# A new pacing condition for the expert-weight loads: from scatters sent to weights split

## The reference

```
logits = xf @ w_cls.T ; scores = softmax(logits)          # 32 routed experts + 32 that do nothing
topk_idx = top_k(scores + bias, 8) ; w = scores[topk] / sum * 1.5
for each routed expert e (at most 256 tokens of its own):
    g, u = split(x_e @ w_gate_up[e])                        # 512 -> 2 x 256
    y_e  = (silu(g) * u) @ w_down[e]                        # 256 -> 512
out[token] += w * y_e[token] * (1 + weight of the experts that do nothing)
```

## Time and profile before

| what | value |
|---|---|
| profiled execution, its own time | 969.67 us |
| its span | 967.9 us |
| mean granted TensorE clock | 0.98 of full speed |
| DMA moved over the span | 127.06 MB |
| HBM read, written | 106.53 MB, 32.90 MB |
| VectorE, ScalarE, GpSimd busy | 80%, 52%, 50% of the span |

### The profile page before, as it was taken

How to read it: one execution, slowest core, us unless ns; L and a number is a source line. 1 busy time by engine, 2 the same in 40 slices (tenths; PEclk the granted TensorE clock), 3 DMA queues, 4 the chain that set the end, 5 groups by cost and what they waited for, 6 DMA issues and landing times. The chain is left out here.

```text
span 967.9 us, 14567 instructions
## 1 busy us (share of the span) xinstructions
PE 904.0 (93%) x4362; PEld 731.9 (76%) x4362; DVE 772.4 (80%) x1843; ACT 503.1 (52%) x867; POOL 481.9 (50%) x395
## 2 busy tenths in 40 slices
PE   4789999999999999999988999999997699999995
PEld 3667888888888888888857888888875567777783
DVE  6968888888888898888887777777777598888882
ACT  5445545555545555455565323223322488787782
POOL 2457656667666676566650000000003458688852
PEclk9979999999999999999999999999998799999999
DMA  8001111111111111110275377444228589899932
GB/s 312 6 22 61 39 50 59 46 49 39 61 49 45 49 61 39 50 59 35 83 277 195 123 266 261 143 154 151 70 70 284 155 255 331 280 336 281 323 42 38
DMA packets 67369, 127.06 MB, mean 131 GB/s; under 512 B 12073, under 2 KB 14505, under 8 KB 65233
## 3 DMA queue, kind: packets, MB, share of 16 engines
q1 hardware_dynamic: 58144, 114.67, 33.8%
q0 software_dynamic: 9136, 11.31, 6.4%
HBM read 106.53 MB, written 32.90 MB: 144 GB/s over the span
## 5 line engine op out<-in xcount | busy, mean ns | idle before, releaser
L595 POOL TENSOR_TENSOR a_t<-a_t 128x512 f32<-128x512 f32 x80 | 105.0, 1313 | 102.8 <-DVE a_t L358 102.8
L604 POOL TENSOR_TENSOR a_fQ<-a_fQ,a_den 128x512 f32<-128x512 f32 x64 | 87.9, 1374 | 71.9 <-DVE a_den L396 71.9
L213 PE MATMUL a_PQ<-w_h,a_xT_h 128*128 128x512 f32 x384 | 107.8, 403 | 10.3 <-DVE w_l L345 9.6
L782 PE MATMUL r_PY<-w_h,r_o_h 128*128 128x512 f32 x256 | 105.8, 413 | 3.4 <-DVE r_o_l L884 3.4
L1070 POOL TENSOR_SCALAR r_vr<-r_mv 128x1 f32<-128x1 f32 x16 | 8.4, 525 | 196.7 <-DVE r_mv L895 196.7
L213 PE MATMUL a_PQ<-w_l,a_xT_h 128*128 128x512 f32 x384 | 105.3, 397 | 0.0
L213 PE MATMUL a_PQ<-w_h,a_xT_l 128*128 128x512 f32 x384 | 103.4, 391 | 0.0
L1214 POOL DMA_INDIRECT m_xg<-xn2d,si x64 | 81.4, 1272 | 40.3 <-issue 18.2
L782 PE MATMUL r_PY<-w_h,r_o_l 128*128 128x512 f32 x256 | 101.1, 395 | 0.0
L782 PE MATMUL r_PY<-w_l,r_o_h 128*128 128x512 f32 x256 | 100.5, 393 | 0.0
L392 DVE CUSTOM_DVE_ANT_0 a_m<-a_fQ,a_z 128x128 f32<-128x128 f32 x256 | 100.4, 444 | 0.0
(11 more groups left out here) (182 smaller groups left out, 2243.4 us busy)
## 6 DMA issues: line engine op xcount, KB each, us to landing
oT<-a_o SPq DMA_DIRECT2D x64, 256.0 KB, 2.4
v_l<-in_wgu SPq DMA_DIRECT2D x32, 512.0 KB
raw<-in_wgu SPq DMA_DIRECT2D x24, 512.0 KB
v_l<-oT SPq DMA_DIRECT2D x11, 1024.0 KB, 7.0
v_l<-in_wd SPq DMA_DIRECT2D x16, 512.0 KB
raw<-in_wd SPq DMA_DIRECT2D x12, 512.0 KB
v_h<-oT SPq DMA_DIRECT2D x5, 1024.0 KB, 6.1
out<-r_x SPq DMA_DIRECT2D x18, 256.0 KB, 2.0
```

What stands on the lines that cost most here:

```text
L213: last = eng.matmul(bank[:, :], a[:, k, :], w[:, 4 * i + k, :], start=s == 0 and k == 0, stop=s == 2 and k == 3)
L595: eng.tensor_tensor(t1[:, r % 2, :], t1[:, r % 2, :], t2[:, r % 2, :], ALU.add).then_inc(sm["xr"], 1)
L604: eng.tensor_tensor(q, q, den[:, n % 2, :].unsqueeze(2).broadcast_to([P, 4, P]), ALU.mult).then_inc(sm["fs"], 1)
L782: last = eng.matmul(PY[c % 2][:, :], a[:, c % 2, h * P:(h + 1) * P], b[:, h, :], start=h == 0 and s == 0, stop=h == NH - 1 and s == 2)
```

## The change

SyncE no longer waits for `m_sent`, and GpSimd no longer counts it. In its place every part of every load from expert 8 on waits for `m_wl >= 3(e-5) + part + 1`: VectorE has split the same part of expert `e-5`. The waits for the slot's former user stay. Parts, sizes, order and number of the transfers stay.

```
@@ -1192,8 +1192,7 @@
                     for part in range(3):
                         for t in range(2):
                             eng.wait_ge(sm[f"m_gu{t}" if part < 2 else f"m_yd{t}"], e - RING + 1)
-                        if e >= RING + 2:
-                            eng.wait_ge(sm["m_sent"], e - RING - 1)
+                        eng.wait_ge(sm["m_wl"], 3 * (e - RING + 3) + part + 1)
                         if part < 2:
                             load_up(sm, eng, ring, wgu, e, (part,))
                         else:
@@ -1216,15 +1215,14 @@
-                def scatter(e, t, rows, done, last):
+                def scatter(e, t, rows, done):
                     i = 2 * e + t
                     if t == 0 and e >= 1:
                         eng.wait_ge(sm["m_s"], 32 * e)
                     eng.wait_ge(sm[f"m_y{t}"], e + 1)
                     eng.indirect_dma_start(
                         out[:, :], bass.IndirectOffsetOnAxis(ap=si[0:rows, i:i + 1], axis=0),
-                        y[0:rows, e % 4, t, :], None, compute_op=ALU.add,
-                        engine_sem=sm["m_sent"] if last else None).then_inc(sm["m_s"], done)
+                        y[0:rows, e % 4, t, :], None, compute_op=ALU.add).then_inc(sm["m_s"], done)
@@ -1237,10 +1235,10 @@
                     with eng.If_lt(regs[e % 7], T):
-                        scatter(e, 0, P, 16, False)
-                        scatter(e, 1, P, 16, True)
+                        scatter(e, 0, P, 16)
+                        scatter(e, 1, P, 16)
                     with eng.Else():
-                        scatter(e, 0, 64, 32, True)
+                        scatter(e, 0, 64, 32)
```

## The result

The changed kernel takes 978.83 us (median of 4 runs, 972.0 to 981.46); the kernel before, run beside it, 969.08 us (median of 4, 962.09 to 969.67). The ratio of after to before is 1.0119, with a 95% interval of 1.0069 to 1.0169: slower by about 1.2%, where I had forecast 969.4 us and no change. This ratio is not the quotient of the two medians (1.0101): it rests on 20 executions of the changed kernel, 971.63 to 984.93 us, with a 21st of 986.47 us left out as slow. The ratios of the experiments are formed in the same way, each against the kernel before as it ran beside them. The profiled execution took 979.09 us, its span is 977.3 us.

A forecast was written before the change was run, and what follows sets the result against it. The bound was a 5.58 us ring of dependences per expert iteration, without transfers, nearly filled by TensorE's work. From 969.67 us, minus 0, 0, 0 and 0.3, came 969.4 us; range 966.8 to 971.8.

The forecast's parts named there:

- I take 0 for the increment: GpSimd's scatters lose the `m_sent` increment: cost 0, at most a few hundredths of a microsecond for each of 32 scatters.
- the 4.89 us between scatters 8 and 9: On GpSimd, scatter 9 starts 4.89 us after scatter 8, read as released by scatter 8's landing.
- 0.69 us to spare: Slack per expert claimed for the chain of scatters: the iteration's 5.58 us minus 4.89.
- Rival C: Scatters fall behind as spread parts lengthen landings by 1.5 us, until `y` buffers run out: 972.5 us, chance 0.13.
- The page estimate: Scatters meeting HBM's loaded latency, 1.8 us more each, would give 979.1 us; given a small part of Rival C's chance.
- The removed wait of SyncE: Dropping SyncE's wait for `m_sent`: worth 0 to TensorE, since that queue runs 29 us ahead of its reader.
- The added wait: SyncE's `m_wl` wait delays loads 1.3 to 5 us steadily, up to 19 us at the start; hidden by cover, cost 0.
- The startup: Load 8 leaves the stretch 756 to 760 us, where ScalarE and TensorE idle: gain taken as 0.3 us.
- rival B: Without load 8 the startup's 2.50 us "remote" wait shrinks, TensorE resumes up to 2.7 us sooner: 967.0 us, chance 0.20.
- The sign that I had set: Prediction is wrong if the iteration's length changes at all or the stretch 750 to 780 changes by over 1.9 us.

The follow-up runs named there:

- e3_counted: The changed kernel, but its scatters still count `m_sent`, for which nobody waits: 965.88 us, ratio 0.998.
- e1_both: The kernel before with the new `m_wl` wait added to the old `m_sent` wait: 965.16 us, ratio 0.9987.
- e9_counted_nopace: The kernel before without any pacing wait on SyncE, its scatters still counting `m_sent`: 961.47 us, ratio 0.9979.
- e7: The kernel before with the scatter's two waits swapped, so the landing wait is an instruction of its own: 974.65 us, ratio 1.0152.
- e5: The changed kernel with `m_sent` still counted and the scatter's two waits swapped, the landing wait its own instruction: 986.76 us, ratio 1.0279.
- e10_even_counted: The changed kernel, but only scatters of even experts count `m_sent`, for which nobody waits: 967.13 us, ratio 1.0017.

## Why the prediction was wrong

**The step that failed** is "On GpSimd the scatter loses one increment and keeps its descriptors ... I take 0 for the increment". Its bound, a few hundredths of a microsecond for each scatter, priced the increment as work. As work it costs nothing that can be seen: the last scatters take 1.43 us with it and without. What it does is let a scatter of 64 rows go without the wait for `m_s` that is on it. Without it, each scatter is held for the landing before, 3.84 us behind its predecessor at the end instead of 2.10. That turned a chain that follows the copies into one of 5.7 to 7.5 us a step beside an iteration of 5.58.

**The reading under it failed too.** I took the 4.89 us between scatters 8 and 9 in the earlier trace rows as a landing, since the bracket names one. But scatter 9 starts 0.86 us after its copy ends, as scatter 31 does after its own (0.81 us, with nothing landed). The timeline of ACT before:

```profile
825.15 0.60 ACT L1415 ACTIVATE m_y<-m_PY 128x512 f32<-128x512 f32 x1
```

The copies of experts 8 and 9 are 5.84 us apart (819.31 and 825.15), and scatter 8 lagged 0.95 us more behind its copy (1.81 us, behind a gather) than scatter 9. 5.84 minus 0.95 are the 4.89 us, and the "0.69 us to spare" of the landing chain was a number of nothing. The real step under load stood in none of my rows, because the counted scatters don't show it.

**Rival C had the path and not the cause.** I gave it 0.13 and priced it at 972.5 us. It named the resource that ran out, the four `y` buffers. It left the lag 15.0 us to grow; measured it grew by 18.3, from 4.2 to 22.5, with iterations that had grown longer by then. Its rate was close: 0.81 us per expert forecast, measured (22.5 minus 4.2) over the 17 experts from 2 to 19, which is 1.08. Its mechanism was wrong: not a landing that grows because the parts lie over the scatters (e3_counted has the same parts and no loss) but the landing being waited for at all. And its price left out two followers: the gathers behind the scatters on GpSimd, which cost TensorE 8.0 us of waits where `y` cost ScalarE 3.4, and the 5.2 us at the end, which are paid whatever the slack.

**The page estimate** of 979.1 us by the Trainium skill (DMA: Bandwidth & Descriptors, section Latency and other measured facts) lies 0.3 us from the median and is right by luck: it needs a rise of the landing time from the one pacing to the other, and e3_counted shows no loss from the pacing.

**The removed wait of SyncE**, taken at 0 because its reader is 29 us behind: right in this kernel (e1_both, e3_counted and e9_counted_nopace are all at 1.00). It is right only because the scatters ran free. With a real landing wait the same removal costs 1.3% (e7 against e5). I had argued from the load's cover alone and not from what else a held load may do, for which the likely candidate is to leave the DMA engines to the scatter.

**The added wait**, steady and at the start, taken at 0: right, with its times to 0.2 us. **The startup**, 0.3 us or rival B's 2.7: the steady part of the changed kernel starts 5.7 us earlier, but the load is not the reason. Some 2.4 us of it lie ahead of everything that the change touches: the first gather of the experts starts at 736.16 us after and at 738.54 before. The wait that rival B wanted shortened stands in e3_counted, where load 8 goes out at 774.03 and not in this stretch (timeline of ACT):

```profile
757.68 0.60 ACT L1379 ACTIVATE m_xT_h<-m_PX 128x512 fp32r<-128x512 f32 x1 [2.45 <-remote]
```

Before, it was 2.50 us. And the pair of scatters of expert 1 comes at 780.10 us before, at 780.03 in e3_counted, which has the new issues, and at 770.08 in e7, which has the old ones. What sets this stretch stays open; each is one execution. The sign that I had set, that the prediction is wrong if the stretch from 750 to 780 changes by over 1.9 us, was met, but not through the change.

**What stays open**: how the wait for `m_s` is dropped, by the chip or by what loads the program onto it, why the one for `m_y1` is not, and whether it always is. One counted scatter of the kernel before, that of expert 2 at 789.36, stood for 2.83 us and started 2.9 us behind its copy, which I can't explain. It is no accident of one execution: the same scatter stands 1.36 us in e1_both, 1.84 in e3_counted, 2.70 in e9_counted_nopace and 1.48 in e10_even_counted. It is the first scatter of 64 rows and follows a pair of 128; there the wait may have held. Seen are the start of the scatter, its packets and the time. The landing wait is there to keep two scatters from adding to the same row at once. At the end of the kernel before the packets of scatter 31 still come after all 80 of scatter 30; whether that always holds under load, with rows shared by neighbouring experts, was not tried. So the kernel before and all that are as fast owe part of their time to a safeguard that is written down and not kept; the changed kernel keeps it.

## What to carry to other kernels

An increment or a wait on an instruction is not priced by its own duration: before one is removed, look whether the instructions that carry it behave like those that don't, here whether the scatter starts before its predecessor's packets have landed. A releaser named beside a short idle time is a guess; check it against the other input of the instruction (a constant 0.8 us behind the copy says copy) and against the packets. And when something in an in-order queue falls behind by a constant amount per iteration, the price is what runs out first, the buffers, the queue's other work and the end, each by itself.

## What the runs showed of the hardware

An accumulating scatter of 64 rows by GpSimd that carries a wait for the landing semaphore and, beside its landing increment, a second increment by the engine, started though the wait was not met: 2.10 us behind its predecessor, against 3.83 to 3.95 us without that increment. A scatter of 128 rows with the second increment that carries a wait for a semaphore of ScalarE did wait: it started 0.27 us after the copy. The Trainium skill (Perfetto Trace Analysis, section DMA Instruction — SWDGE (GPSIMD)) lists the semaphores being satisfied before such an instruction goes to its engine; the kernels without the second increment agree (3.84 us), those with it do not where the wait is for the landing. The same section says that whether surplus semaphore updates are supported there is not known; here the kernels with one ran, and the wait for the landing was what gave way.

With the DMA engines otherwise idle, a scatter held for the landing of one of 64 rows of 2 KB starts about 3.8 us behind it: the first packet moves some 2.0 us after the start, and the packets then take some 1.0 to 1.3 us. Beside full weight loads the held scatters follow one another mostly by 5.7 to 7.5 us.
